# A fused attention stage on one Trainium2 core: the scores moved to the end of TensorE's step, two copies moved to VectorE, and GpSimd's step reordered

## The reference

```python
# first layer, for each of 16 batches of 128 x 256
h = layernorm(x)                                    # mean and variance over 256
q, k, v = h @ Wq.T + bq, ctx @ Wk.T + bk, ctx @ Wv.T + bv     # 16 heads of 16
w = softmax(where(mask == 0, -1e9, q k^T / 4))
y = w v + ctx
x = x + layernorm(y) * gamma + beta
# mixture of experts: 8 experts, 2 for each row
n = layernorm(x)
score = n @ Wr.T + br
idx = top_k(score + biases, 2)
x = x + sum over the 2 chosen experts of their weight * expert(n)
```

## Time and profile before

| what | value |
|---|---|
| median of 3 runs | 971.3 us (967.41 to 971.63) |
| the profiled execution: its time | 964.62 us |
| its span, first to last instruction | 962.8 us |
| TensorE busy over the span | 863.3 us (90%) |
| VectorE, ScalarE, GpSimd busy | 593.4, 466.4, 384.8 us |
| first layer's attention | from the start to about 205 us |
| mean granted TensorE clock | 0.971 |

### The profile page before, as it was taken

One profiled execution on the slowest core, in us unless ns is written; L12 is line 12 of the kernel. 1 busy time (PEld: TensorE's weight loads), 2 busy tenths in 40 slices (PEclk: granted clock), 3 DMA queues, 4 the chain that ended last, 5 costly groups with the idle time before them and its releaser, 6 DMA issues. The chain is left out here.

```text
span 962.8 us, 26663 instructions
## 1 busy us (share of the span) xinstructions
PE 863.3 (90%) x9044; PEld 730.8 (76%) x9045; DVE 593.4 (62%) x1484; ACT 466.4 (48%) x1194; POOL 384.8 (40%) x610
## 2 busy tenths in 40 slices
PE   5888888759999999997999989999999999679995
PEld 4676776429999999995556678888888887568784
DVE  3587886544545455552027467768668787459995
ACT  3788787412222222221343435445554454359895
POOL 4488886620000000005201346445464454336662
PEclk9999999979999999999999999999999999889998
DMA  6445656342433333315765687777776875212111
GB/s 170 121 157 163 187 162 213 139 153 89 128 99 95 95 108 94 100 41 190 266 223 147 152 171 169 148 160 154 161 156 145 162 159 125 58 41 63 58 59 45
DMA packets 190187, 128.27 MB, mean 133 GB/s; under 512 B 128544, under 2 KB 175648, under 8 KB 189984
## 3 DMA queue, kind: packets, MB, share of 16 engines
q1 hardware_dynamic: 155728, 93.72, 37.8%
q10 hardware_dynamic: 31312, 25.17, 9.1%
q0 software_dynamic: 3072, 8.39, 2.7%
HBM read 78.25 MB, written 48.99 MB: 132 GB/s over the span
## 5 line engine op out<-in xcount | busy, mean ns | idle before, releaser
L1745 ACT ACTIVATE c_pT<-c_T 128x512 f32<-128x512 f32 (+2 forms) x90 | 50.2, 595 | 103.5 <-PE c_T L1905 72.9
L1689 POOL TENSOR_TENSOR c_soft<-c_soft,c_share 128x616 f32<-128x616 f32 (+2 forms) x96 | 70.4, 761 | 60.0 <-DVE c_share L2161 58.4
L1080 ACT ACTIVATE b_rowsT<-b_RT 128x256 f32<-128x256 f32 x39 | 15.0, 384 | 158.2 <-PE b_RT L1122 158.2
L1699 POOL MEMSET d_round<- 128x1 f32 x1 | 0.1, 98 | 227.3 <-POOLq L970 227.3
L1194 DVE COPY b_w<-moe_w 128x1024 f32 x78 | 53.6, 688 | 52.9 <-issue 47.5
L1131 PEld LDWEIGHTS b_G<-b_rowsT,b_w 128*128 128x128 f32 x624 | 77.2, 196 | 4.5 <-DVE b_w L1194 2.2
L1131 PE MATMUL b_G<-b_rowsT,b_w 128*128 128x128 f32 x624 | 78.0, 280 | 1.7 <-DVE b_w L1194 0.9
L1208 DVE SCALAR_TENSOR_TENSOR b_hidT<-b_U,b_bias,b_gate 128x128 f32<-128x128 f32 x156 | 43.9, 344 | 55.6 <-PE b_U L1131 55.6
L1131 PE MATMUL b_U<-b_rowsT,b_w 128*128 128x128 f32 x624 | 76.6, 277 | 0.0
L1158 PE MATMUL b_Y<-moe_w,b_hidT 128*128 x312 | 73.9, 380 | 0.9 <-DVE b_out L1239 0.9
L1131 PEld LDWEIGHTS b_U<-b_rowsT,b_w 128*128 128x128 f32 x624 | 73.4, 194 | 0.0
(11 more groups left out here) (241 smaller groups left out, 2056.9 us busy)
## 6 DMA issues: line engine op xcount, KB each, us to landing
moe_w<-in_L_Wl SPq DMA_DIRECT2D x16, 512.0 KB
rel_windows<-c_relw ACTq DMA_DIRECT2D x28, 276.0 KB, 5.1
c_bias<-rel_windows SPq DMA_DIRECT2D x16, 462.0 KB, 5.0
prob_rows<-c_soft SPq DMA_DIRECT2D x16, 462.0 KB, 5.6
early<-in_L_early SPq DMA_DIRECT2D x16, 384.0 KB, 3.2
values<-c_pT ACTq DMA_DIRECT2D x22, 256.0 KB, 2.7
b_rows<-expert_lists SPq DMA_DIRECT2D x39, 128.0 KB, 2.1
expert_out<-b_out SPq DMA_DIRECT2D x39, 128.0 KB, 1.7
```

The costliest lines, as they stand in the source:

```text
L1689: ins = nc.gpsimd.tensor_tensor(soft[p][:, hs, a:z], soft[p][:, hs, a:z], share[:, s, hs].unsqueeze(2).to_broadcast([P, HS, z - a]), ALU.mult)
L1745: nc.scalar.activation(dst, view(T[k]), ACT.Copy, **kw).then_inc(g["emptied"], 1)
```

## The change

There are three parts, all in `layer0`.

1. TensorE: `scores` is issued at the end of the step before (for b+1, behind `values(b+1)`), and `transposes` for b+1 comes near the start of a step in place of that for b+2 at the end. `places` comes first, `attention` behind the first `probabilities`, and `next_rows` behind the third. In the last step `places(15)` is ahead of the text product.
2. VectorE takes the evacuation of the queries (two 128x128 operations) and the fourth copy of the transposed weights (`last_probs`, 128x512) from ScalarE. Its first half of the maxima is now ahead of `rows_normal` and `list_slots`, and `norm_rows` is at the end of the step.
3. GpSimd makes the deviations of kinds 0 and 1 in one pair of instructions on 128x2 (`both_std`), drops a wait on `p_sb`, and issues `listing` and `scatter` one step later than before (for b-4, not b-3), behind both deviations, the masks and the additions.

```diff
             def steps(b, i, p):
-                if there(b + 3):
+                if there(b + 3) and there(b - 2):
+                    both_std(b + 3, b - 2)
+                elif there(b + 3):
                     std(0, b + 3)
-                if there(b - 2):
+                elif there(b - 2):
                     std(1, b - 2)
...
                 if there(b + 2):
                     masks(b + 2, i + 1, p)
-                if there(b - 2):
+                if there(b - 2) and not late:
                     std(2, b - 2)
                 if there(b - 1):
                     residual(b - 1, i - 1 + p, 1 - p)
-                if there(b - 3):
-                    if there(b - 1):
-                        apart(pool, g["p_sb"], 4 * (b - 1) + HPT)
-                    scatter(b - 3, 1 - p)
-                    listing(b - 3, 1 - p)
+                if there(b - 4):
+                    listing(b - 4, p)
+                    scatter(b - 4, p)
...
+            def both_std(ahead, behind):
+
+                apart(pool, g["var1"], behind + 1)
+                apart(pool, g["var"], ahead + 1)
+                links[0].begin(ahead)
+                links[0](nc.gpsimd.tensor_tensor(rstd[:, 0:2, 0], agg[:, 0:2, 1], eps[:, :], ALU.add))
+                nc.gpsimd.tensor_tensor(rstd[:, 0:2, 1], rstd[:, 0:2, 0], shared["mhalf"][:, :].to_broadcast([P, 2]), ALU.pow)\
+                    .then_inc(g["rstd"], 1)
...
+            def queries(b):
...
+                for m in range(KD):
+                    ins = nc.vector.tensor_scalar(qT[:, m, :], M[0][:, m * P:(m + 1) * P], bq[:, m:m + 1], SCALE0, ALU.add, ALU.mult)
+                ins.then_inc(g["q_sb"], 1)
+
+            def last_probs(b):
+
+                dve.wait_ge(g["p_mm"], 4 * b + HPT)
+                since(dve, g["pv_mm"], b)
+                nc.vector.tensor_copy(pT[HPT - 1][:, :, :], M[1][:, :].rearrange("p (m n) -> p m n", m=MT0)).then_inc(g["p3_sb"], 1)
```

More of the change, by code:

```diff
@@ L547, in steps @@
                 if there(b - 1):
-                    for k in range(2):
+                    for k in range(HPT - 1):
                         probs(b - 1, k)
@@ L551, in steps @@
                     next_rows(b - 3)
-                if there(b - 1):
-                    for k in range(2, HPT):
-                        probs(b - 1, k)
                 if there(b):
[L556 to L560, removed]
+                    for h in range(2):
+                        exps(b, p, h)
                 if there(b - 1):
@@ L711, in _ @@
             values(0, 0)
-            transposes(1, 1)
+            scores(0, 0)
             def steps(b, i, p):
+                if there(b - 4):
+                    places(b - 4, p)
+                if there(b + 1):
+                    transposes(b + 1, 1 - p)
+                if there(b - 1):
+                    probabilities(b - 1, 1 - p, 0)
                 if there(b - 2):
                     attention(b - 2)
-                if there(b - 4):
-                    places(b - 4, p)
                 if there(b - 1):
[L720 to L724, removed]
+                    for k in (1, 2):
+                        probabilities(b - 1, 1 - p, k)
                 if there(b - 3):
@@ L727, in steps @@
                 if there(b - 1):
-                    for k in range(2, HPT):
-                        probabilities(b - 1, 1 - p, k)
+                    probabilities(b - 1, 1 - p, 3)
+                if there(b + 1):
+                    queries(b + 1, 1 - p)
                 if there(b - 3):
@@ L738, in steps @@
                     values(b + 1, 1 - p)
-                if there(b + 2):
-                    transposes(b + 2, p)
+                    scores(b + 1, 1 - p)
+                if isinstance(b, int) and b == NB + 2:
+                    places(b - 3, 1 - p)
                 if isinstance(b, int) and b >= NB:
                     text_values(text_halves(b))
-                if isinstance(b, int) and b == NB + 2:
-                    places(b - 3, 1 - p)
             by_batch(steps)(pe)
@@ L880, in _ @@
             norm_in(1, 0, 1)
+            queries(0)
             dve.wait_ge(s_wk, 32)
@@ L913, in steps @@
                     out_var(rows)
-                if front:
-                    norm_rows(b + 3, 1 - p)
+                if ahead:
+                    queries(b + 1)
                 if rows_ready:
@@ L919, in steps @@
                     keys(b + 1, 1 - p)
+                if behind:
+                    rows = rows_scaled(b - 2)
                 if rows_ready:
@@ L926, in steps @@
                 if behind:
-                    rows_out(b - 2, i - 1, p, rows)
                     rows_stats(b - 2, p)
+                if front:
+                    norm_rows(b + 3, 1 - p)
             by_batch(steps)(dve)
```

81 lines of the change are left out of this document (43 added, 38 removed).

## The result

The changed kernel takes 1033.3 us (median of 4 runs, 1032.05 to 1043.03), the kernel before 969.4 (median of 4). The ratio is 1.068 (95% interval 1.0645 to 1.0716): slower by 64 us on the medians. The profiled execution took 1034.08 us with a span of 1032.2, against 964.62 and 962.8 before, so 69.5 us more; the profiled execution of before lay 4.7 us under the median of its 4 runs.

A forecast was written before the change was run, and what follows sets the result against it. A chain between engines was taken to bound the kernel at 10.17 us a step. Ring 54, drain 10.5, start -5 and clock 10 sum to +70: 1034 us on the profiled execution, 1041 from the median 971.3; range 1012 to 1076.

The forecast's parts named there:

- What bounds the kernel before: First layer's loop: no engine is full; a chain between engines sets the step of 10.17 us.
- part 1: Scores a step early, two copies moved to VectorE: 9.0 to 9.2 us a step by TensorE and VectorE, gain 1.0 to 1.1.
- the ring: Wait chain within a step: rows_normal, VectorE, GpSimd's third deviation, additions, listing, scatters, landing, rows_normal again; 12 rounds, +54 us.
- The ring's length: One round from rows_normal to the next: VectorE 7.0, GpSimd's terms and a landing of 3.0 sum to 14.7 us, against 10.17.
- The landing: Time from the second scatter's issue until its data lands: 3.0 us taken, between 2.5 quiet and 3.9 in the loop.
- The clock: TensorE's two pauses a round lower its clock and delay the keys: 0.7 us in 14 rounds, +10 (0 to +36).
- rival A: TensorE's clock is down in every round, +36 in place of +10: 1067 us, up to 1075; chance 0.25.
- Start, drain and end: Steps 0 to 4 gain 5 us, the two drain rounds add 10.5, the end with places(15) and text adds 0.
- The signs: Trace marks: VectorE idle 3 to 5 us ahead of L858, steps of 14 to 16, GpSimd idle over 5 ahead of L428.
- B: Rival: rounds close sooner, with landing 2.5 us, full clock and a larger gain at the start; 1022 us, chance 0.14.
- C: Rival: the scatter's landing does not hold rows_normal, steps fall to VectorE's 9.1 to 9.2 us; 956 us, chance 0.05.
- D: Rival: longer waiting and the gains of part 1 balance, so no change; needs a round near 10 us; chance 0.01.

The follow-up runs named there:

- scatter back: On the changed kernel, listing and scatter are issued for b-3 again, still behind the additions, the rest of the change kept; 956.5 us, ratio 0.989.
- additions last: On the changed kernel, GpSimd's two additions are moved behind the scatter, as the last call of its step; 1037.5 us.

## Why the prediction was right

- **What bounds the kernel before, and part 1.** Right in kind, too large in size. With the scatter back VectorE is the fullest engine, but a round falls only from 10.18 to 9.77 us (0.4; over 12 rounds 0.7), where 1.0 to 1.1 was forecast. It is 0.6 over the 9.1 to 9.2 of the engines alone; from step 3 to step 6 its rounds took 9.1 us, and the later ones about 10. This miss did not reach the total, since the ring hides part 1's gain.
- **The scatter is in a ring.** Shown: adding it alone costs 80 us (1046.7 against 966.9), removing it alone gives back 77.
- **The ring's length.** 14.7 summed, 14.3 in the step at full clock and 14.63 with the pauses filled. No single term was off by over 0.3 us in the step that I read. That the mean of 12 rounds came out right as well (+63.0 for 62.6) is in part luck. Against the terms of the sum the landing cost 5 us more than forecast (3.4 a round for 3.0), VectorE's part, which the clock stretches, 2.4 less (6.2 above the full-clock sum, for 8.6), and GpSimd 2.4 less (4.5 a round for 4.7).
- **The landing.** I took 3.0, and the mean is 3.4. That the scatter would come "nearer to quiet" was only half right: with the weights loaded late the landing falls to 2.5 us, and in one of the 12 rounds, behind the text's loads, it took 6.4. That those loads make it so is read from the order of the issues; no run takes them away.
- **The clock.** The size was about right (10 us forecast; 7 us came back on the medians with 28 transposes in the pauses) and it is shown that a low clock lengthens the ring. My argument against rival A, that the first pause is well under 3.53 us, was wrong: the clock fell within a pause of 2.78 us, and right after one of 2.97 us. Rival A itself (1067, the clock down in every round) is out, since two rounds ran at 1.00 throughout.
- **Start, drain and end.** -2.5 for -5, +7.2 for +10.5, -1.0 for 0. In the drain VectorE's part took 5.4 and 5.8 us where 6.9 was taken for both rounds. For the start I had given steps 0 to 4 a gain from the beginning, but `rows_normal` of steps 3 and 4 only shows 9.11 us a step (43.84 to 52.95) after a start that gained little.
- **The signs.** The second scatter went out 11.57 us after L858 (11.5 foretold), and GpSimd idled 5.7 to 8.4 us ahead of L428 in the eight rounds from step 5 on. VectorE's idle time was foretold wholly ahead of L858, 3 to 5 us; it is split, mostly 1.5 to 3.0 there and 2.4 to 3.1 ahead of L886, for `places`.
- **The total.** +70 forecast on the profiled execution's time, +69.5 measured. So close a fit is luck: the drain came out 4.7 us under its forecast with its share of the clock, and the smaller gain at the start (2.5) and the later stages (2.7) made up for it. On the medians it is +64, because the 964.6 of the profile lay below its own median; added to 971.3 the same sum read 1041 instead of 1033.
- **Rivals.** B (1022) is out by 11 us. C is excluded as stated, since L858 waits for the DMA in all rounds from step 5. D is out too, since no round from step 4 to step 16 was under 13 us and D needs about 10.

## What to carry to other kernels

Before an issue is moved behind another wait, write down who waits for its end and how many steps lie between; a buffer that two steps of distance made free becomes a ring when the distance falls to one, and its length is a plain sum over the engines' rows. Look for the second ring too (here 11.9 us, and in another order 10.5), because mending the first ring gains no more than down to the second. A gain on one term of a ring can be lost on another: here 1.4 us of additions left it, and the landing, issued nearer to the weights, took 1.4 us more. A sum read from one step has to be held against the mean of all rounds, where one slow landing (6.4 us) counts.

## What the runs showed of the hardware

- The granted clock of TensorE fell from 1.00 to 0.50 within a pause of 2.78 us (it was 0.50 from 111.5 on, ahead of the matmul at 111.87), and a pause of 2.62 us in the same kernel (ended at 126.42) did not lower it. 28 transposes a step that nothing reads held it at 1.00 from 52 to 170 us, but not through the wait of 6.5 us that followed, and brought the kernel from 1033.3 to 1026.1 us.
- An indirect scatter of 128 KB landed 2.4 to 2.5 us after its issue in eight rounds of the changed order with no weight loads in the steps, 3.9 us after it when it went out 1.6 us behind 768 KB from SyncE's queue (additions last), and 6.4 us after it when it went out 2.3 us behind another 1.5 MB (the changed kernel).
- On GpSimd the pow on 128x2 took 0.71 to 0.73 us, against 0.57 on 128x1.
- The unrolled steps took 1030.2 us, 3 us less than with the hardware loop (1033.3).
